# Products of sums and reciprocals on GpSimd in the second attention, and folding transposes placed among the next block's maxima

## The reference

```
x = x + L0_xattn(layernorm(x), ctx)      # 16 heads of 16, biases, mask
x = x + L0_ffn(layernorm(x))             # 6 experts, top 2
x = x + L1_xattn(layernorm(x), ctx)      # 16 query heads, one shared k and v
x = x + L1_ffn(layernorm(x))             # 256 -> 1024 -> 256, fixed-point, piecewise-linear gelu

# L1_xattn
qh = (q @ w_q).reshape(B, L, 16, 16).transpose(0, 2, 1, 3)
k, v = split(c @ w_kv)
attn_prob = softmax(einsum('bhid,bjd->bhij', qh, k) / sqrt(16))
out = einsum('bhij,bjd->bhid', attn_prob, v).transpose(0, 2, 1, 3).reshape(B, L, D) @ w_concat
```

## Time and profile before

| | us |
|---|---|
| median of 3 runs | 918.43 (917.15 to 921.13) |
| the profiled execution | 921.4 |
| its span in the profile | 919.6 |
| PE busy | 799.4 (87%) |
| DVE busy | 655.0 (71%) |
| ACT busy | 519.6 (56%) |
| POOL busy | 380.0 (41%) |
| second attention, from the start of block 8 (465.3) to the first step of the last layer (655.7) | 190.4 |

### The profile page before, as it was taken

How to read it: one execution, slowest core, us unless ns; L and a number is a source line. 1 busy time by engine, 2 the same in 40 slices (tenths; PEclk the granted TensorE clock), 3 DMA queues, 4 the chain that set the end, 5 groups by cost and what they waited for, 6 DMA issues and landing times. The chain is left out here.

```text
span 919.6 us, 13728 instructions
## 1 busy us (share of the span) xinstructions
PE 799.4 (87%) x4452; PEld 587.1 (64%) x4452; DVE 655.0 (71%) x1576; ACT 519.6 (56%) x942; POOL 380.0 (41%) x323
## 2 busy tenths in 40 slices
PE   4699999999859999999878888888788988899994
PEld 3456656666548877777645454555567877787784
DVE  6567777777747778777857888887576776767573
ACT  4255555555344455544256666666467766776772
POOL 3622332221233443443202221221378766776782
PEclk9889999999989999999879999998889999999998
DMA  9755754335100000010555555551000000000001
GB/s 285 119 102 103 137 92 82 79 74 103 46 0 1 1 6 1 1 47 1 69 71 70 71 69 103 67 70 23 1 1 1 24 24 1 24 23 24 1 25 46
DMA packets 24817, 48.01 MB, mean 52 GB/s; under 512 B 3655, under 2 KB 6856, under 8 KB 24234
## 3 DMA queue, kind: packets, MB, share of 16 engines
q1 hardware_dynamic: 22792, 42.87, 25.6%
q10 hardware_dynamic: 1954, 4.26, 1.3%
HBM read 11.47 MB, written 4.19 MB: 17 GB/s over the span
## 5 line engine op out<-in xcount | busy, mean ns | idle before, releaser
L299 ACT ACTIVATE pt<-bank 77x512 f32<-77x512 f32 x256 | 146.1, 588 | 125.7 <-PE bank L397 76.2
L325 DVE TENSOR_REDUCE mx<-bank 128x4 f32<-128x308 f32 x256 | 110.0, 472 | 38.5 <-PE bank L372 25.0
L394 PE MATMUL bank<-qst,l_kst 128*77 128x512 f32 (+1 forms) x256 | 107.7, 436 | 19.6 <-DMA qst<-mt 13.2
L694 POOL TENSOR_TENSOR fy<-fpart,fg 128x512 f32<-128x512 f32 x64 | 89.7, 1401 | 46.3 <-DVE fpart L735 41.0
L369 PE MATMUL bank<-l_kblk,qh 128*128 128x308 f32 x256 | 91.4, 372 | 14.8 <-DVE mx L325 13.5
L687 POOL TENSOR_TENSOR frise<-fg,fg 128x512 f32<-128x512 f32 x64 | 86.5, 1351 | 17.7 <-POOL fy L694 14.9
L394 PEld LDWEIGHTS bank<-qst,l_kst 128*77 128x77 f32 (+1 forms) x256 | 37.1, 150 | 84.5 <-issue 48.8
L103 POOL TENSOR_TENSOR rstd<-var,minus_half 128x4 f32<-128x4 f32 x32 | 32.7, 1022 | 139.4 <-DVE var L98 90.3
L369 PEld LDWEIGHTS bank<-l_kblk,qh 128*128 128x128 f32 x256 | 50.6, 198 | 57.9 <-issue 50.6
L275 POOL TENSOR_TENSOR ol<-ot,oh 128x512 fp32r<-128x512 f32 x32 | 43.2, 1349 | 98.3 <-ACT oh L304 63.7
L595 DVE SCALAR_TENSOR_TENSOR x<-bank,eweight,x 128x256 f32<-128x256 f32 x192 | 79.6, 476 | 5.4 <-PE bank L627 5.1
(11 more groups left out here) (179 smaller groups left out, 2190.3 us busy)
## 6 DMA issues: line engine op xcount, KB each, us to landing
qst<-qh SPq DMA_DIRECT2D x64, 256.0 KB, 6.6
qst<-ql SPq DMA_DIRECT2D x32, 256.0 KB, 9.4
out<-x SPq DMA_DIRECT2D x8, 512.0 KB, 2.6
qst<-ml SPq DMA_DIRECT2D x8, 480.0 KB
x<-in_x ACTq DMA_DIRECT2D x3, 1024.0 KB, 11.0
weights<-in_mlp_w SPq DMA_DIRECT2D x2, 1024.0 KB, 5.0
mraw<-in_mask SPq DMA_DIRECT2D x8, 154.0 KB
x<-in_x SPq DMA_DIRECT2D x2, 512.0 KB, 5.7
```

What stands on the lines that cost most here:

```text
L299: self.nc.scalar.activation(self.pt[0:T, i // 4 % 2, i % 4, :], self.bank_of(G, i)[0:T, :], ACT.Exp).then_inc(self.probs, 1)
L325: self.nc.vector.reduce_max(out, banks[u % len(banks)][:, 0:4 * T].rearrange("q (p par t) -> q p par t", p=2, par=2), AX.X).then_inc(self. ...
L394: last = self.nc.tensor.matmul(out, layer.kst[rows, layer.stack(c * HC + 2 * k + par), b * T:(b + 1) * T], self.qst[rows, self.slot(G), c ...
L694: self.nc.gpsimd.tensor_tensor(self.y[:, k % 2, :], self.part[:, k % 2, :], self.g0[:, k % self.R, :], ALU.add).then_inc(self.y_ready, 1)
```

## The change

For the second attention only, `divide` is split. DVE keeps `invert` (the transpose to `ut` and the reciprocal), POOL gets the product, `quotient`. Three things move:

- the product of every quarter goes from DVE to POOL's list: (p, 3) at the head of block G, before `norm.invert`; (G, 0), (G, 1), (G, 2) at its end, behind the weights' low parts; (15, 3) ahead of the last two `rest_quotient`;
- `fold(p, 1)` stands behind the maxima 4, 5, 6 instead of ahead of them, and `fold(G, 0)` behind `norm.rest` instead of ahead of it; both wait for POOL's products now (`divided`);
- `invert(G, q)` waits until the product of quarter q-2 has been made, since it writes the same slot of `ut`. The product waits for `fold` of block G-1 of its half.

The first attention still calls `divide`, which is `invert` and `multiply` on DVE as before.

```
+    def quotient(self, pool, G, q):
+        self.multiply(pool, self.nc.gpsimd, G, q)
+        pool.wait_ge(self.divided, 4 * G + q + 1)
...
+    def invert(self, dve, G, q):
         k = 4 * G + q
         dve.wait_ge(self.weighed, k + 1)
+        need(dve, self.divided, k - 1)
+        self.nc.vector.transpose(self.ut[:, q % 2, :], self.U[:, :]).then_inc(self.unfolded, 1)
...
+    def multiply(self, who, engine, G, q):
+        c, par = divmod(q, 2)
+        who.wait_ge(self.inverse_ready, 4 * G + q + 1)
+        need(who, self.folded, C * (G - 1) + c + 1)
+        group = self.ut[:, q % 2, :].rearrange("p (j d) -> p j d", d=32)
+        engine.tensor_tensor(self.o32[:, c, :, par, :], group[:, :, 0:DH],
+                             self.rden[:, q % 2, :, :].to_broadcast([P, N // 32, DH]), ALU.mult).then_inc(self.divided, 1)
...
                 for G in range(BLOCKS, 2 * BLOCKS):
+                    if G > BLOCKS:
+                        att.quotient(pool, G - 1, 3)
                     norm.invert(pool, LN_ATT1 + G - BLOCKS + 2)
...
+                    for q in range(3):
+                        att.quotient(pool, G, q)
+
+                att.quotient(pool, 2 * BLOCKS - 1, 3)
...
                     if p >= BLOCKS:
-                        att.divide(dve, p, 3)
+                        att.invert(dve, p, 3)
+                    if n < 2 * BLOCKS:
+                        att.take_maxima(dve, n, range(4, 7), att.X)
+                    if p >= BLOCKS:
                         att.fold(dve, p, 1)
                     if n < 2 * BLOCKS:
-                        att.take_maxima(dve, n, range(4, 10), att.X)
-                    att.divide(dve, G, 0)
+                        att.take_maxima(dve, n, range(7, 10), att.X)
+                    att.invert(dve, G, 0)
...
-                    att.divide(dve, G, 1)
-                    att.fold(dve, G, 0)
+                    att.invert(dve, G, 1)
                     if nm <= LN_FFN:
                         for c in range(C):
                             norm.rest(dve, nm, c, ...)
-                    att.divide(dve, G, 2)
-                att.divide(dve, 2 * BLOCKS - 1, 3)
+                    att.fold(dve, G, 0)
+                    att.invert(dve, G, 2)
+                att.invert(dve, 2 * BLOCKS - 1, 3)
```

More of the change, by code:

```diff
@@ L326, in take_maxima, with divide @@
                                       AX.X).then_inc(self.max_taken, 1)
-    def divide(self, dve, G, q):
-        nc = self.nc
-        c, par = divmod(q, 2)
+    def invert(self, dve, G, q):
         k = 4 * G + q
         dve.wait_ge(self.weighed, k + 1)
-        nc.vector.transpose(self.ut[:, q % 2, :], self.U[:, :]).then_inc(self.unfolded, 1)
+        need(dve, self.divided, k - 1)
+        self.nc.vector.transpose(self.ut[:, q % 2, :], self.U[:, :]).then_inc(self.unfolded, 1)
         dve.wait_ge(self.unfolded, k + 1)
         group = self.ut[:, q % 2, :].rearrange("p (j d) -> p j d", d=32)
[L336 to L339, removed]
+        self.nc.vector.reciprocal(self.rden[:, q % 2, :, :], group[:, :, DH:DH + 1]).then_inc(self.inverse_ready, 1)
+    def multiply(self, who, engine, G, q):
[5 more added lines that the diff above has]
+                             self.rden[:, q % 2, :, :].to_broadcast([P, N // 32, DH]), ALU.mult).then_inc(self.divided, 1)
+    def divide(self, dve, G, q):
+        self.invert(dve, G, q)
+        self.multiply(dve, self.nc.vector, G, q)
     def fold(self, dve, G, c):
```

## The result

The change makes the kernel slower: 933.27 us (median of 4 runs, 932.29 to 935.32) against 917.99 (917.15 to 921.13), a ratio of 1.0163 with a 95% interval of 1.0133 to 1.0193. That is 15.3 us more; 13.1 were forecast. The profiled execution took 932.29 us, its span is 930.5.

What follows compares the result with a forecast made beforehand. The prediction took a chain through several engines as the bound, DVE's saved time counting only on it. Terms 9.8 + 1.7 - 0.5 + 1.3 + 0.8 = 13.1 on 918.4 gave 931.4 us, range 924 to 938.

Steps and rivals of the forecast that it cites:

- Rival (a): DVE is the bound, so taking its 32 products away makes the kernel faster, 18 us less, 900 us; chance 0.04.
- (c): POOL's product is slow, 1.28 us, so terms 1, 2 and 4 grow by some 10: 941 us; chance 0.10.
- (b): No change: term 1 mostly hidden, term 2 repaid by contention that goes, 922 us; chance 0.09.
- (d): Only the stalls cost: `ol` isn't late and part of a stall is hidden, 7 us more, 925; chance 0.10.
- Term 1: Blocks 9, 10, 12, 13: DVE's fold waits for POOL's products behind the weights' low parts; four stalls, +9.8 us.
- Term 5: TensorE's clock: pauses from the four stalls drop it to the lower level, 0 to 1.6 us, half taken, +0.8.
- Term 2: Blocks 9 to 14: POOL's longer chain to `ol` delays output; +1.7 in 11 to 14, -0.5 in 9 and 10.
- Term 3: The fold moved behind maxima 4 to 6 costs 0, its place hidden by `ol`; otherwise worth 0.06 a block.
- Term 4: The ends: block 8 -0.4, block 15's output waiting for POOL +1.3, the last fold +0.4; together +1.3 us.

Runs made afterwards that it cites:

- experiment 2: The changed kernel with ScalarE making the second high part of the weights behind exponential 8 instead of 14 in blocks 9, 10, 12 and 13: 918.84 us.
- experiment 7: Products (G, 0), (G, 1) put back behind both weight halves, in a 912.32 us kernel with them between, norm first, fold behind maxima 4 and 5: 924.36 us.
- experiment 1: The changed kernel with POOL making products (G, 0) and (G, 1) between the two weight halves in blocks 9, 10, 12 and 13: 918.83 us.
- experiment 5: As experiment 1, with only fold(p, 1) moved to behind maxima 4 and 5: 917.43 us.
- Experiment 6: The kernel before the change, products on VectorE, with only fold(p, 1) moved behind maxima 4 and 5: 913.87 us.
- experiment 8: As experiment 7, with PE repeating scores where it would wait behind the stalls, the real scores overwriting them: 920.83 us.
- experiment 11: PE repeats in blocks 8 and 11, added to a 910.64 us kernel (products between weight halves, norm first, earlier fold, block 15 reordered): 908.44 us.

## Why the prediction was right, and where not

**The mechanism** was right. The four stalls are where it put them, behind the second low parts, with VectorE's fold as the waiting step: idle times of 3.93, 3.94, 3.24 and 3.24 where 3 to 4 were named. The product took 0.62 where 0.65 was taken and 0.64 to 1.28 were the bounds; the row with the broadcast operand was the right neighbour. Rival (a) falls with the result, (c) with this row, and (b) came true only where experiment 2 made its condition. (d) falls with the late output and with stalls of 8.6 and not 7, but half of it was right: the stalls are all that is left in the total. The first output product waits for `ol` 0.44 to 0.51 in four of the blocks 9 to 14, 0.06 in block 11 and not at all in block 14.

**Term 1, +9.8: 8.6.** The four stalls of the working add up to 9.7. The steps from `fw1l` to the fold held within 0.07. In blocks 9 and 10 a stall is worth 2.5 and not 2.8, in 12 and 13 1.8 and not 2.06. The step that was off is the way from the fold to the first maximum, 4.65 measured, 4.85 in the working: both `ql` run at one go now, 1.28, since `qh` had long been there.

**Term 5, the clock, +0.8: 3 to 6.** This is the term that was mis-sized. I took the one dip of the earlier trace rows at 0.4, and half of four of them. All four came in experiment 7's trace. In the changed kernel's, two came behind a stall, from 547 and from 625, and the second lasted 10 us. Two more stand elsewhere: one from 554, and the one from 605, which comes 12 us behind its stall and 7 behind block 13's first maximum, where experiment 1 has one without any stall. Such a stretch costs more at most places: 1.2 and 0.9 in experiment 7, 1.4 and 1.3 in experiment 1, and in the changed kernel's own trace 13-14, with a stretch at 606, is 1.3 longer than 12-13 without one. Why the one in the earlier trace rows cost only 0.4 wasn't tried. How the 3 to 6 us of the changed kernel spread over its blocks isn't shown: only four executions of it were timed and one was traced. The error of this term has the opposite sign to those of terms 1 and 4, and the total came out 2 us short of 15.3. So the mechanism was no luck, but that the total is so near is partly luck: term 1 is 1.2 too large, what stands beside stalls and clock about 2.5 too large by experiment 1, and the clock 2 to 5 too small.

**Term 2, the way to `ol`, +1.2: right in size.** Output begins 6.07 and 5.97 behind `ut` where 5.99 was worked out. In the table, experiment 5 against before has +0.3 in 12-13 and 13-14, and -0.5 and -0.4 in 9-10 and 10-11, where the meeting with GpSimd went (+0.4 and -0.25 in the working, which took 0.6 for the late output there and not its own 0.4; with 0.4 it is -0.45). In 11-12 it has -1.2, but there the kernel before has a half-clock stretch (from 560) and experiment 5 none.

**Term 3, the moved fold, 0: right here, wrong beyond.** As long as `ol` is late, its place is worth nothing: experiments 1 and 5 differ by 0.9. But "if `ol` came sooner, it would be worth 0.06 a block" was wrong: it is 1 us a block. I counted the maxima in pairs and left out that PE's list has the weighing between the tiles 5 and 6. So there is a hole behind maximum 5, and a fold behind 6 splits a pair.

**Term 4, the ends, +1.3.** Block 15 was right: after, the output stands 2.21 for `ol`, 5.97 behind `ut(14, 3)` at 648.23.

```profile
654.20 0.36 PE L431 MATMUL bank<-l_woh,oh 128*128 128x256 f32 x1 [2.21 <-POOL ol L275]
```

14-end costs 1.9 to 2.0 in experiments 5 and 1, 2.1 in the working with block 14's share. Block 8 is where the term failed: from its first `xl` to the first maximum of block 9 are 30.1 before and 28.4 in experiments 1 and 5, 1.7 less and not 0.4. There too it goes with the clock: before has a stretch of 6.8 us at the lower level (478 to 485), experiment 1 one of 3.4 (479 to 482). Experiment 6, whose block 8 is that of the kernel before, has such a stretch too (477 to 484) and 30.1. The ends are then near zero together, which is most of why experiment 1 comes out at nothing. In the changed kernel's own trace they are -0.6 (29.5, with the lower level until 472) and +2.9.

The Trainium skill, GPSIMD Engine Reference, 4.1 Engine selection, has GpSimd about 2 times slower for two inputs. The trace says less for this product of 128x256, 0.62 against 0.42 to 0.43, 1.46 times. So the product alone was no reason against the change. What counted was where it stood in the list.

## What to carry over

An engine that is two fifths busy isn't free: what counts is whether its list, in order, has a step that waits long for another engine, and who waits for the work queued behind that step. Put the price of a stall together from two parts, the time itself, and the TensorE clock behind it, here 3 to 6 us on 8.6. Where two ways to the same instruction are equally long, an edit that shortens one shows nothing; try the pair before dropping either.

## What the runs showed of the hardware

- PE's granted clock fell to the lower level after slices in which PE was busy 0.38 or 0.39 of 2 us, in the changed kernel also after two slices of 1.23 and 1.19, and did not fall where repeats of a product filled the same place to 1.80. Work whose result is thrown away took 3.5 us off the median in experiment 8 and 2.2 in experiment 11. A product of 512 columns takes 0.23 from start to start at 2.4 GHz and 0.43 at 1.2 GHz.
- VectorE's product of two operands in SBUF took 0.42 alone and 1.13 to 1.27 when it met one of GpSimd's subtractions, and ended 0.27 and 0.28 us behind it. The Trainium skill, SBUF — State Buffer, Who interferes with whom, has a VectorE instruction with two inputs in SBUF contend with a GpSimd instruction that reads SBUF, over a shared pair of ports that only one of the two holds at a time; the trace agrees, in that the product ended behind the subtraction each time.
